# First graph convolution: part of the edge rows is made by TensorE from a node table in SBUF instead of being gathered

## The reference, cut to what matters

```python
h = x @ W
s = jnp.concatenate([src, loop]); d = jnp.concatenate([dst, loop])
deg = jax.ops.segment_sum(ones, d); dinv = rsqrt(deg)
out = jax.ops.segment_sum(h[s] * (dinv[s] * dinv[d])[:, None], d) + b
...
x = gcn_conv(node_features, W1, b1, src, dst); x = relu(x)
x = gcn_conv(x, W2, b2, src, dst)
```

## Time and profile before

| | |
|---|---|
| median of 3 runs | 4342.69 us (4335.5 to 4344.24) |
| profiled execution, span | 4341.1 us; a time of its own beside the span is not listed |
| first convolution: first gather, last sum stage on DVE | 126.8 us, 1119.5 us |
| second convolution: first gather, last gather | 1124.4 us, 2101.3 us |
| busy over the span | PE 63%, DVE 49%, ACT 26%, POOL 60% |

### The profile page before, as it was taken

One profiled execution on the slowest core, in us unless ns is written; L12 is line 12 of the kernel. 1 busy time (PEld: TensorE's weight loads), 2 busy tenths in 40 slices (PEclk: granted clock), 3 DMA queues, 4 the chain that ended last, 5 costly groups with the idle time before them and its releaser, 6 DMA issues. The chain is left out here.

```text
span 4341.1 us, 48722 instructions
## 1 busy us (share of the span) xinstructions
PE 2731.0 (63%) x12610; PEld 2187.4 (50%) x12610; DVE 2147.7 (49%) x4371; ACT 1116.2 (26%) x2854; POOL 2600.8 (60%) x2731
## 2 busy tenths in 40 slices
PE   5333433333344444334599899777778777767998
PEld 4333333333344443333488444456666666646776
DVE  7422222222322222222677444378888888874666
ACT  6111111111111111111155222244444444425222
POOL 6677777777677777777533422177777777742000
PEclk9655665566666556655699999878888888875999
DMA  4522222222322221222389554444444444430000
GB/s 125 117 55 53 53 53 53 53 53 58 86 53 53 53 53 53 53 53 53 103 262 303 194 200 179 161 136 139 137 136 141 136 136 141 136 122 23 17 22 21
DMA packets 217305, 437.05 MB, mean 101 GB/s; under 512 B 54179, under 2 KB 128291, under 8 KB 210244
## 3 DMA queue, kind: packets, MB, share of 16 engines
q0 software_dynamic: 102016, 246.46, 20.9%
q1 hardware_dynamic: 84164, 150.77, 9.9%
q10 hardware_dynamic: 30848, 36.54, 2.9%
HBM read 332.04 MB, written 107.31 MB: 101 GB/s over the span
## 5 line engine op out<-in xcount | busy, mean ns | idle before, releaser
L1431 POOL DMA_INDIRECT ring<-t_gcn,idx x1564 | 1480.2, 946 | 499.4 <-issue 476.4
L1505 PE MATMUL psum<-ring,big 128*128 x3328 | 752.6, 418 | 1175.0 <-SPq L1441 1166.7
L1505 PEld LDWEIGHTS psum<-ring,big 128*128 128x128 f32 x3328 | 701.2, 321 | 1218.5 <-issue 1218.5
L1817 POOL DMA_INDIRECT xs_ring<-t_msg,idx x832 | 799.7, 961 | 380.5 <-issue 249.4
L1537 DVE TENSOR_TENSOR big<-big,psum 128x1024 f32 x208 | 254.0, 1221 | 1428.7 <-PE psum L1505 1427.6
L1464 ACT COPY psum<-zero_sum 128x1024 f32<-128x1024 f32 x208 | 211.0, 1015 | 1334.8 <-DVE big L1537 1316.8
L1950 PE MATMUL psum<-xs_ring,a_hot 128*128 128x264 f32 x1456 | 409.9, 442 | 0.0
L1950 PEld LDWEIGHTS psum<-xs_ring,a_hot 128*128 128x128 f32 x1456 | 332.1, 228 | 75.8
L1704 PE MATMUL psum<-big,a_xnt 128*128 128x512 f32 x784 | 354.0, 594 | 0.5 <-ACT a_xnt L1676 0.5
L222 DVE TENSOR_TENSOR big<-dloc,psum 128x1024 f32<-128x1024 f32 x208 | 252.5, 1214 | 4.4 <-PEq L705 4.3
L2083 DVE TENSOR_TENSOR xs_ring<-xs_ring,psum 128x2048 f32<-128x2048 f32 x104 | 235.9, 2269 | 0.9 <-ACT psum L1876 0.9
(11 more groups left out here) (445 smaller groups left out, 4430.6 us busy)
## 6 DMA issues: line engine op xcount, KB each, us to landing
t_msg<-a_rows SPq DMA_DIRECT2D x49, 1056.0 KB
big<-t_w ACTq DMA_DIRECT2D x105, 256.0 KB
a_near<-t_near SPq DMA_DIRECT2D x52, 512.0 KB, 4.2
ring<-t_gcn,idx POOLq DMA_INDIRECT x1564, 2.5
ring<-t_tok SPq DMA_DIRECT2D x105, 128.0 KB, 3.8
t_y<-ring SPq DMA_DIRECT2D x105, 128.0 KB, 3.7
xs_ring<-t_msg,idx POOLq DMA_INDIRECT x832
xs_ring<-in_x SPq DMA_DIRECT2D x7, 896.0 KB, 11.7
```

What stands on the lines that cost most here:

```text
L1431: g.indirect_dma_start(out=ring[:, p % HALF_RING * 8 + j, :], out_offset=None, in_=t_gcn[conv], in_offset=bass.IndirectOffsetOnAxis(ap=idx ...
L1505: m = t.matmul(opened[:, bass.ds(to[j], ROW_BYTES)].bitcast(F32), hot[q % 2][:, j, :], ring_bytes[:, bass.ds(at[j], ROW_BYTES)].bitcast(F3 ...
L1817: g.indirect_dma_start(out=ring[:, slot, :, :].rearrange("p h c -> p (h c)"), out_offset=None, in_=t_msg, in_offset=bass.IndirectOffsetOnA ...
```

## The change

In the first convolution every tenth group of tiles or so is no longer gathered. The 782 tiles are cut into periods of 36: four bunches of eight, which POOL gathers as before, and one of four (a quad). The quads from the second period on, 20 of them or 80 tiles, are made on chip:

- SP loads the whole node table into SBUF at the start (49 blocks of 128 nodes, 512 bytes per row).
- For each quad ACT loads the sources of its 512 edges, broadcast to all partitions; DVE and ACT each keep a copy.
- For each of the 49 node blocks a comparison tile of 128 x 512 is built: one where the edge's source is that node, else zero. DVE builds three of five (one `is_equal`), ACT two of five (Abs, then Relu of one minus it). There are five buffers.
- PE multiplies the block's rows with the comparison tile and sums over the 49 blocks in PSUM, which gives the quad's rows, transposed. ACT copies them to SBUF, PE transposes them back, and ACT copies them into the ring slots where the gather would have put them.
- The 980 block matmuls stand behind the steps of turns 1 to 90, 98 per nine turns.

The bunches, 109 instead of 98, hold for both convolutions; in the second all are gathered. The tables `fetch` and `freed` are computed for them with some more small instructions. ACT now clears the sums one turn earlier in its queue. The addition of `b2` is cut into seven pieces in turns 91 to 97.

```diff
+PERIOD = RING // 2
+QUAD = 4
+PLACES = 10
+BUNCHES = [(PERIOD * q + 8 * j, min(8 if j < 4 else QUAD, ET - PERIOD * q - 8 * j))
+           for q in range(-(-ET // PERIOD)) for j in range(5) if PERIOD * q + 8 * j < ET]
+QUADS = len(BUNCHES) // 5 - 1
+BLOCKS = QUADS * NT
+HOTS = 5
...
-                    v.tensor_scalar(fetch[:], slot[:].rearrange("p (q s) -> p q s", s=GROUP)[:, :, GROUP - 1], 3, None,
-                                    ALU.arith_shift_right).then_inc(c.sem, c.up())
+                    v.tensor_scalar(period, last_of, 1821.0, None, ALU.mult).then_inc(c.sem, c.up())
...
+                    v.tensor_scalar(period, period, 16, None, ALU.arith_shift_right).then_inc(c.sem, c.up())
...
+                    v.scalar_tensor_tensor(fetch[:], period, -float(PERIOD), last_of, ALU.mult, ALU.add).then_inc(c.sem, c.up())
...
+                    v.tensor_scalar(fetch[:], fetch[:], 3, None, ALU.arith_shift_right).then_inc(c.sem, c.up())
...
+                    v.scalar_tensor_tensor(fetch[:], period, 5.0, fetch[:], ALU.mult, ALU.add).then_inc(c.sem, c.up())
...
+                    def by_pool(i):
+                        return not helped or i % 5 < 4 or i < 5
...
+                        def by_scalar(b):
+                            return b % HOTS in (1, 3)
...
+                        def turn_of(b):
+                            return 1 + 9 * b // 98
...
+                            table = t_gcn[conv].rearrange("(n p) f -> p n f", p=P)
+                            sp.dma_start(near_rows, table[:, 0:near_blocks, :]).then_inc(s_rows_in.sem, 16)
+                            sp.dma_start(far_rows[:], table[:, near_blocks:NT, :]).then_inc(s_rows_in.sem, 16)
+                        for i in range(len(BUNCHES)):
+                            if by_pool(i):
+                                sp.wait_ge(s_row[i % PLACES].sem, s_row[i % PLACES].base + landed_by[i])
+                            else:
+                                sp.wait_ge(s_helped.sem, s_helped.base + i // 5)
                             sp.sem_inc(s_c.sem, 1)
...
+                        def one_hot(b):
+                            k, n = divmod(b, NT)
+                            if b >= HOTS:
+                                a.wait_ge(s_block.sem, s_block.base + b - HOTS + 1)
+                            a.activation(one_of[b % HOTS][:], src_kept, ACT.Abs, bias=minus_nid[:, n:n + 1]).then_inc(s_abs.sem, 1)
+                            a.wait_ge(s_abs.sem, s_abs.base + ones_by(b, True))
+                            a.activation(one_of[b % HOTS][:], one_of[b % HOTS][:], ACT.Relu, bias=unit[:], scale=-1.0).then_inc(s_one_a.sem, 1)
+
+                        def flatten(k):
+                            a.wait_ge(s_block.sem, s_block.base + (k + 1) * NT)
+                            if k:
+                                a.wait_ge(s_upright.sem, s_upright.base + k)
+                            a.copy(turned_rows[:], quad_place(k)).then_inc(s_flat.sem, 1)
+
+                        def put_back(k):
+                            first_tile = BUNCHES[5 * k + 9][0]
+                            at = first_tile % RING
+                            a.wait_ge(s_upright.sem, s_upright.base + k + 1)
+                            if first_tile >= RING:
+                                a.wait_ge(s_used.sem, s_used.base + GROUP * ((first_tile - RING + QUAD + NT - 2) // GROUP + 1))
+                            a.copy(ring[:, at:at + QUAD, :], quad_place(k).rearrange("p (t f) -> p t f", f=HID)).then_inc(s_helped.sem, 1)
...
+                        def block(b):
+                            k, n = divmod(b, NT)
+                            if b == 0:
+                                t.wait_ge(s_rows_in.sem, s_rows_in.base + 32)
+                            if n == 0 and k >= 2:
+                                t.wait_ge(s_helped.sem, s_helped.base + k - 1)
+                            if by_scalar(b):
+                                t.wait_ge(s_one_a.sem, s_one_a.base + ones_by(b, True))
+                            else:
+                                t.wait_ge(s_one_v.sem, s_one_v.base + ones_by(b, False))
+                            rows = near_rows[:, n, :] if n < near_blocks else far_rows[:, n - near_blocks, :]
+                            t.matmul(quad_place(k), rows, one_of[b % HOTS][:], start=n == 0, stop=n == NT - 1,
+                                     skip_group_check=True).then_inc(s_block.sem, 1)
+
+                        def tensor_help(q):
+                            for b in turn_blocks.get(q, []):
+                                block(b)
+                            if q in uprights:
+                                k = uprights[q]
+                                t.wait_ge(s_flat.sem, s_flat.base + k + 1)
+                                for j in range(QUAD):
+                                    m = t.transpose(quad_place(k)[:, j * P:(j + 1) * P], turned_rows[:, j * P:(j + 1) * P], ident[:])
+                                m.then_inc(s_upright.sem, 1)
...
+                        ADDED_AT = 2 * TURNS - 13
...
+                                if not by_scalar(b):
+                                    if b >= HOTS:
+                                        v.wait_ge(s_block.sem, s_block.base + b - HOTS + 1)
+                                    v.tensor_scalar(one_of[b % HOTS][:], src_place, nid[:, n:n + 1], None, ALU.is_equal).then_inc(s_one_v.sem, 1)
...
-                            if conv == 0 and q == 2:
-                                v.wait_ge(s_act.sem, s_act.base + 1)
-                                v.tensor_tensor(xs[:], xs[:], ps[4][:, 0:D].unsqueeze(1).to_broadcast([P, NT, D]), ALU.add).then_inc(s_dve.sem, 1)
-                                v.wait_ge(s_dve.sem, s_dve.base + 1)
+                            if helped:
+                                vector_help(turn_blocks.get(q, [])[0:HOTS])
+                            if conv == 0 and 0 <= q - ADDED_AT < NG:
+                                w = slice((q - ADDED_AT) * GT, (q - ADDED_AT + 1) * GT)
+                                v.tensor_tensor(xs[:, w, :], xs[:, w, :], ps[7][:, P:P + D].unsqueeze(1).to_broadcast([P, GT, D]), ALU.add).then_inc(s_dve.sem, 1)
...
                             v.tensor_tensor(nodes_at, nodes_at, sums(q), ALU.add).then_inc(s_added.sem, 1)
+                            if helped:
+                                vector_help(turn_blocks.get(q, [])[HOTS:])
```

More of the change, by code:

```diff
@@ L525, in _ @@
                     v.memset(zero_sum[:], 0.0).then_inc(c.sem, c.up())
-                    v.memset(freed[:, 0:HALF_RING - 1], 0).then_inc(c.sem, c.up())
-                    v.tensor_copy(freed[:, HALF_RING - 1:HALVES], krow[:, 0:(HALVES - HALF_RING + 1) * 8].rearrange(
-                        "p (h s) -> p h s", s=8)[:, :, 0]).then_inc(c.sem, c.up())
+                    v.memset(freed[:, 0:PLACES], 0).then_inc(c.sem, c.up())
+                    for j in range(5):
+                        end = 8 * j + 8 if j < 4 else PERIOD
+                        many = len(range(PLACES + j, len(BUNCHES), 5))
+                        v.tensor_copy(freed[:, PLACES + j:len(BUNCHES):5], krow[:, end:end + PERIOD * (many - 1) + 1:PERIOD]).then_inc(c.sem, c.up())
                     v.memset(big[:, NT * HID:(NT + GROUP - 1) * HID], 0.0).then_inc(c.sem, c.up())
@@ L1423, in _ @@
                         freed_at = g.alloc_register(f"freed_at{conv}")
-                        for p in range(HALVES):
-                            if p >= HALF_RING:
-                                g.load([freed_to], freed[0:1, p:p + 1])
+                        for i, (first_tile, many) in enumerate(BUNCHES):
+                            if not by_pool(i):
+                                continue
+                            if i >= PLACES:
+                                g.load([freed_to], freed[0:1, i:i + 1])
                                 g.reg_alu(freed_at, freed_to, 0, ALU.max)
@@ L1429, in _ @@
                                 g.nop(nofuse=True)
[L1430 to L1433, removed]
+                            for e in range(first_tile, first_tile + many):
+                                g.indirect_dma_start(out=ring[:, e % RING, :], out_offset=None, in_=t_gcn[conv],
+                                                     in_offset=bass.IndirectOffsetOnAxis(ap=idx1[:, e:e + 1], axis=0)
+                                                     ).then_inc(s_row[i % PLACES].sem, 16)
                         if conv == 1:
@@ L1438, in _ @@
                     def _(sp):
-                        for p in range(HALVES):
-                            sp.wait_ge(s_row[p % HALF_RING].sem, s_row[p % HALF_RING].base + 128 * (p // HALF_RING) + 16 * min(8, ET - 8 * p))
+                        if helped:
[3 more added lines that the diff above has]
+                        for i in range(len(BUNCHES)):
+                            if by_pool(i):
```

(81 more changed lines are left out.)

70 lines of the change are left out of this document (59 added, 11 removed).

## The result

The changed kernel takes 4455.75 us (4454.65 to 4464.31, four runs), the kernel before 4343.42 in the same comparison: a ratio of 1.0267, interval 1.0253 to 1.0282, slower by 112 us. The profiled execution's span is 4452.9 us, 111.8 over that of before.

What follows compares the result with a forecast made beforehand. POOL's gathers, 1.25 us each, were taken to bound the first convolution, and PE after the change. A stage end 108 us later, 18 us of hand-over and 8 us at quads' ends made 134 us on 4341.1: 4475 us, range 4435 to 4570.

Steps and rivals of the forecast that it cites:

- PE becomes the bound: First convolution, to the end of turn 90: PE needs 1009 us, more than POOL's 878 us for 702 gathers.
- Rival 2: First convolution: PE's clock doesn't stay up; at 0.83 its work takes 207 us more, 4656 us plus gaps; 8%.
- the hand-over of 0.2 us per turn: PE's passage to the next turn's register loads, over 89 turns: 0 to 68 us, taken as 18 us.
- The quad's end: ACT copies the result before building its next tile: 0 to 1.2 us per quad, taken as 0.4, 8 us.
- The start: First block at 154.4 us, after turn 1's steps end at 153.4 us and 1 us of added table preparation.
- the first of the two bounds: Node table's load into SBUF at 212 GB/s: 15 us, so no wait; the other bound was 42 us.
- The tail: Turns 91 to 103, without blocks, at DVE's pace: 65 us against 117 before.
- the cover: PE's work hides comparison-tile building, costed at nothing; gone above 1.34 us per DVE tile or 2.15 us per ACT tile.
- rival 3: First convolution: the comparison tiles' makers bind; at 2.5 us per ACT pair 80 us more, 4555 us; 8%.
- Rival 1: First convolution: POOL stays the bound and the change saves its gathers, 4242 us, with blocks at most 0.60 us; 6%.
- The rule: Skill page's 131 ns sustained per 512-column matmul would make a PE block 0.52 us instead of 0.86, with POOL the bound.

Runs made afterwards that it cites:

- the rest of the edit alone: Changed kernel with every tile gathered by POOL in both convolutions, bunches, tables, earlier clears and bias pieces kept: 4336.67 us, ratio 1.0004 to the kernel before.
- the bf16 version: Changed kernel, all twenty quads, rows split into two bf16 parts, two bf16 matmuls per block: 4240.94 us, ratio 0.9782 to the kernel before.
- the run with light makers: Changed kernel, but after the first five tiles DVE and ACT rewrite only 64 of 512 columns: 4444.70 us, ratio 1.0254 to the kernel before.
- the bias run: Changed kernel with the seven b2 pieces in turns 40 to 46 instead of 91 to 97: 4442.65 us, ratio 1.0249 to the kernel before.

## Why the prediction was right, and where its sum was off

*Main step.* "PE becomes the bound" held, and at the price taken from the attention's projection: 0.86 us per block, 1.78 instead of 1.76 us per turn's steps. From the first block to the end of turn 90 the forecast had 1009 us without stalls; the trace has 1015 with all of them. The experiments carry it: halving PE's columns alone turns 112 us lost into 99 saved; lightening the makers alone moves 4 us; the rest of the edit alone moves nothing that shows; ten quads, with PE under POOL, and fifteen, with the two level, save 1.2 us per gather (48 and 74 us).

*Clock.* The granted clock was 1.00 for 900 us. Rival 2's gaps of 3.5 us did not occur; from 180 us to the end of turn 90 PE's longest wait was 1.9 us.

*Mis-sized terms.* The forecast was 134 us, the span moved 111.8. Over-sized was the hand-over of 0.2 us per turn, 18 us: behind 9.4 us of blocks it is nothing (1108.96 us follows its blocks without idle time). The reason given, that long blocks give the loads time, fits: with blocks half as long it was there, 73.7 us in 73 turns. The quad's end was costed at 8 us and shows as PE's 1.9 us of waits for ACT.

The start was put at 154.4 us and came at 150.2, as the table preparation was no later (first gather at 126.9 us), and turn 1's steps began 1.4 us earlier (148.31 us) and ran at the high level already. The second of the two loads of the node table landed 17 us after its issue at 127.6 us, in time and near the first of the two bounds (15 us, not 42). The tail was 64.1 us (1165.2 to 1229.3) for 65 forecast. So 1015 - 1009 = 6 us of stalls came in place of 26, half of them at seven quads' ends (0.43 us each by the starts) and most of the rest waits for landed tiles in the first turns, and with 4 us from the start and 1 from the tail the stage moved 110 where 134 was forecast.

*Makers.* A DVE tile took 0.75 us for 0.69, an ACT pair 1.44 for 1.15. Both still fit 11.2 us a turn (DVE 7.3, ACT 7.3), so the cover held and the errors cost nothing. For rival 3 it would have taken 2.3 us per pair by the prediction's own sum per turn, (11.1 - 1.0) / 4.4; its 2.15 counts neither PE's steps nor the clears.

*Rival 1* needed blocks of at most 0.60 us. With 0.43, in the bf16 version, it came true: POOL set the pace and the saving was 94 us. So its arithmetic was right and its condition was not met by fp32.

*The rule.* The Trainium skill, page "TensorE: Matmul & The Clock Gate", section "Back-to-back issue gap", has about 131 ns sustained and 216 ns isolated for 512 columns. The bf16 blocks here, a stream of weight loads and matmuls at a granted clock of 1.00, were 0.216 us apart, the fp32 instructions 0.429. The trace agrees with the higher figure alone.

## What to carry to other kernels

Work given to an idle-looking engine must be costed with a row of the same shape and type at the clock that it will then run at, and all that this engine already does in the stage at that clock too; the two sums per turn, here 11.2 us on PE against 8.4 on POOL (878 us over 104 turns), tell who is the bound. They must cover the same stretch. When help costs more than it saves, change its amount before dropping it: almost the same code at 15 of 20 quads saved 74 us, and by the sums the best amount is where both meet, which is near 15 here (16 to 19 were not run). Halving one engine's work with all else kept is the quickest proof of which engine pays.

## What the runs showed of the hardware that was not expected

- An activation has a fixed part that halving the columns doesn't halve: 1.15 us for 1024 columns, 0.72 for 512, and 0.35 for 64 in the run with light makers, which is about 0.83 us per 1000 columns and 0.29 us each.

```profile
L1552 ACT ACTIVATE one_of<-one_of,unit 128x64 f32<-128x64 f32 x379 | 131.8, 348 | 12.4
```

- PE's hand-over from one turn to the next costs nothing in some places and about 1 us, with no wait shown, in others. It is nothing behind the changed kernel's full blocks and between two turns of the kernel before at 1018.69 us, the first of them at the low clock level and 3.5 us long. It is 73.7 us in 73 turns behind the half-column blocks. Turns without blocks start 2.93 us apart with four transposes between them (1165.21 to 1168.14) and 2.98 us apart without (the bias run's tail), for 2.2 and 1.8 us of matmuls. A fixed time of some 2.9 us, as an estimate from these distances, for a turn's register loads and matmul issues would fit the turns without blocks, but not the half-column turns (8.6 us apart) by itself. What the hand-over consists of was not tested and stays open.
